# Attention and ternary feed-forward block: q and k projected from two float16 parts, maxima 11 steps ahead of the scores

## What is computed

```python
q, k, v = n @ Wq, n @ Wk, n @ Wv                 # n = layernorm(x), x is (8, 1024, 256)
q, k = rope(q), rope(k)                          # pairs of columns, cos and sin of the position
p = softmax(q @ k.T / sqrt(256))                 # 16 heads, each 1024 x 1024
x = x + layernorm((p @ v) @ Wo)
x = x + layernorm(layernorm(x) @ ternary(W).T * alpha + bias)
```

## Time and profile before

| | before |
|---|---|
| median of 3 runs | 1544.87 us (1544.76 to 1545.48) |
| profiled execution | 1542.89 us, of which the span from first to last instruction is 1540.9 us |
| busy PE / DVE / ACT / POOL | 94% / 88% / 81% / 45% |
| mean granted TensorE clock | 0.979 |

### The profile page before, as it was taken

The page is one execution under the profiler, slowest core; times in us unless marked ns, Lnnn a source line. Parts: engine busy times, 40 slices in busy tenths (PEclk is TensorE's granted clock), DMA queues, the critical chain, the costliest instruction groups (busy, mean ns, idle before and its releaser), DMA issues.

```text
span 1540.9 us, 31812 instructions
## 1 busy us (share of the span) xinstructions
PE 1453.7 (94%) x12182; PEld 481.2 (31%) x12182; DVE 1360.0 (88%) x1565; ACT 1246.7 (81%) x2454; POOL 686.8 (45%) x1115
## 2 busy tenths in 40 slices
PE   6789999999999999999999999999999999999997
PEld 5122322323232332323223232323323232222236
DVE  5788999898989999899998989899998989999924
ACT  2078888888988888888888889888888888989881
POOL 4214074544636355453735446363554535333240
PEclk9589999999999999999999999999999999999999
DMA  3411111312031121312112120301212120220101
GB/s 106 116 26 56 62 28 61 81 46 69 27 101 27 60 57 44 94 33 74 26 61 81 47 69 27 104 24 60 57 46 65 33 78 22 61 50 17 40 16 52
DMA packets 72919, 84.89 MB, mean 55 GB/s; under 512 B 17632, under 2 KB 58464, under 8 KB 71328
## 3 DMA queue, kind: packets, MB, share of 16 engines
q1 hardware_dynamic: 71952, 82.08, 18.8%
q10 hardware_dynamic: 816, 0.79, 0.2%
HBM read 46.66 MB, written 24.64 MB: 46 GB/s over the span
## 4 chain that ended last, share of the span: by engine, by line
PE 46%; DVE 38%; POOL 7%; ACT 4%; issue 3%; DMA 1%; SPq 0%; POOLq 0%; DVEq 0%; ACTq 0%
DVE row_max L1161 31%; PE smax L933 16%; PE pv L955 14%; PE ring L1053 4%; PE ring L1026 4%; ACT probs L835 3%; PE ring L1061 2%; PE ring L1041 2%; PE ring L979 2%; POOL act L423 2%; POOL res L503 2%; DVE sy_bn L1141 1%; PE ring L1003 1%; DVE max_parts L1179 1%; POOL sa_rs L398 1%
## 5 line engine op out<-in xcount | busy, mean ns | idle before, releaser
L1161 DVE TENSOR_REDUCE row_max<-smax 128x1 f32<-128x1024 f32 x1024 | 1206.2, 1215 | 108.5 <-PE smax L933 105.7
L835 ACT ACTIVATE probs<-ring 128x512 f32<-128x512 f32 x2048 | 1104.6, 597 | 167.2 <-PE ring L979 153.3
L933 PE MATMUL smax<-k_rows,q_rows 48*128 48x512 f16 x2048 | 629.4, 389 | 50.3 <-DVE row_max L1161 40.3
L979 PE MATMUL ring<-q_rows,k_rows 50*128 50x512 f16 x2048 | 634.2, 383 | 0.5 <-ACT probs L835 0.2
L955 PE MATMUL pv<-probs,v_cols 128*32 128x256 f32 (+1 forms) x6240 | 603.5, 459 | 4.1 <-ACT heads L889 3.7
L933 PEld LDWEIGHTS smax<-k_rows,q_rows 48*128 48x128 f16 x2048 | 116.7, 94 | 550.7 <-DVE row_max L1161 291.0
L955 PEld LDWEIGHTS pv<-probs,v_cols 128*32 128x32 f32 x6240 | 123.2, 108 | 307.3 <-issue 163.2
L979 PEld LDWEIGHTS ring<-q_rows,k_rows 50*128 50x128 f16 x2048 | 132.2, 93 | 45.1 <-ACT probs L835 39.8
L535 POOL TENSOR_TENSOR attnT<-pairs,inv_rows 128x512 f32<-128x512 f32 x31 | 39.4, 1271 | 235.3 <-DMA inv_rows<-inv_sums_dram 235.3
L514 POOL TENSOR_TENSOR act<-act,bias_sb 128x256 f32<-128x256 f32 x60 | 42.3, 727 | 80.1 <-ACT act L878 80.1
L1026 PE MATMUL ring<-xT,wq_sb 128*128 128x256 f32 x256 | 71.9, 407 | 5.1 <-ACT rot_in L820 5.1
(11 more groups left out here) (155 smaller groups left out, 1099.0 us busy)
## 6 DMA issues: line engine op xcount, KB each, us to landing
q_stage_dram<-q_parts SPq DMA_DIRECT2D x45, 256.0 KB, 2.5
q_rows<-q_stage_dram SPq DMA_DIRECT2D x30, 384.0 KB, 7.8
x_in<-in_L_attn_x SPq DMA_DIRECT2D x8, 1024.0 KB, 6.1
pairs<-heads SPq DMA_DIRECT2D x64, 128.0 KB
inv_rows<-inv_sums_dram SPq DMA_DIRECT2D x32, 256.0 KB
res<-in_L_attn_x SPq DMA_DIRECT2D x16, 512.0 KB, 5.6
out<-res SPq DMA_DIRECT2D x15, 512.0 KB, 3.2
k_rows<-k_stage_dram SPq DMA_DIRECT2D x64, 96.0 KB, 3.3
```

Source lines behind the costliest of these rows:

```text
L835: eng.activation(probs[:, s % PSLOTS, j, :], ring[:, n % RING, :], ACT.Exp, scale=score_unit).then_inc(ring_read, 1)
L933: mm = eng.matmul(smax[:, side, c, :], q_rows[at:to, qc, kv * KVP + jp, qt * P:(qt + 1) * P], k_rows[at:to, kv, c * 512:(c + 1) * 512], st ...
L979: eng.matmul(ring[:, n % RING, :], k_rows[at:to, g, kt * P:(kt + 1) * P], q_rows[at:to, h.qc, g * KVP + j // 2, :], start=True, stop=True)\
L1161: eng.tensor_reduce(row_max[:, g % 2, at:at + 1], smax[:, side, :, :].rearrange("p c n -> p (c n)"), AX.X, ALU.max).then_inc(max_read, 1)
```

## The change

- The x of each batch (scaled by 1024) and the weights of q and k (scaled by 64) are split into two float16 parts (`x_parts`, `wq_parts`, `wk_parts`), on POOL: four `split_x` in steps 1 to 4 of each `qc` 0 half, `split_weights` once. `Q` and `K` are sums of three float16 products (`PRODUCTS`), in jobs of 512 columns: two `Q` jobs, in steps 16 and 30, instead of four in 4 to 7, and one `K` job in step 6 instead of two in 14 and 15.
- q is rotated at step 8 of the half that follows its projection, staged at step 14 and loaded at 16 of that same half.
- `LEAD` is 11, so `TURN` is 6: `MT` stands in steps 6, 14, 22 and 30.
- The cast of `act_parts` goes from DVE to POOL. The first operation of `split_max` becomes a `scalar_tensor_tensor` with a tile of zeros. The moments of x are taken two in a step (0 to 3), those of y all in step 16, and those of the forward result in 27 and 30.

```diff
-LEAD = 12
+LEAD = 11
 TURN = (-LEAD) % KT + 1
...
 PRO = {0: [("XT", 0, 0)], 1: [("XT", 1, 0)], 2: [("XT", 0, 1)], 3: [("XT", 1, 1)],
-       4: [("Q", 0, 0, 0)], 5: [("Q", 0, 0, 1)], 6: [("Q", 0, 1, 0)], 7: [("Q", 0, 1, 1)],
-       14: [("K", 0)], 15: [("K", 1)]}
+       6: [("K",)], 16: [("Q", 0, 0)], 30: [("Q", 0, 1)]}
...
-        4: [("Q", 1, 0, 0)], 5: [("Q", 1, 0, 1)], 6: [("Q", 1, 1, 0)], 7: [("Q", 1, 1, 1)]}
+        16: [("Q", 1, 0)], 30: [("Q", 1, 1)]}
...
-X_MOM_FIRST, X_MOM = (0, 1, 2, 5, 6, 7, 8, 8), (0, 1, 2, 3, 4, 5, 6, 7)
-A_MOM, Y_MOM, F_MOM = (9, 10, 11, 12), (15, 15, 16, 16), (27, 27, 29, 30)
+X_MOM_FIRST, X_MOM = (0, 1, 2, 5, 6, 7, 8, 8), (0, 0, 1, 1, 2, 2, 3, 3)
+A_MOM, Y_MOM, F_MOM = (9, 10, 11, 12), (16, 16, 16, 16), (27, 27, 30, 30)
...
-K_SWAP = 17
+K_SWAP = 18
...
-Q0_STAGE, Q1_STAGE, Q_LOAD = 30, 30, 6
+Q_STAGE, Q_LOAD, Q_LOAD_FIRST = 14, 16, 6
...
+        def split_x(eng, h, n):
...
+            eng.tensor_copy(hi, src).then_inc(x_high, 1)
+            eng.wait_ge(x_high, before + 1)
+            eng.tensor_tensor(lo, src, hi, ALU.subtract).then_inc(x_parted, 1)
...
-        def split_act(eng, nth, dt):
-
+        def split_act(eng, h, nth, dt):
+
+            eng.wait_ge(ring_read, h.done("HT", dt))
+            eng.tensor_copy(act_parts[:, 0, dt, :], actT[:, dt, :]).then_inc(act_part, 1)
...
+                        for k, (xm, wm) in enumerate(PRODUCTS):
+                            for dt in range(DT):
+                                mm = eng.matmul(dst[:, :], wq_parts[:, wm, dt, a[1], :], x_parts[:, xm, dt, at:at + HALF],
+                                                start=(k + dt == 0), stop=(k == len(PRODUCTS) - 1 and dt == DT - 1))
...
-                eng.tensor_scalar(m1, rows, 1.0 / ROW_UNIT, None, ALU.mult).then_inc(max_split, 1)
+                eng.scalar_tensor_tensor(m1, rows, 1.0 / ROW_UNIT, zeros[:, :, :], ALU.mult, ALU.add).then_inc(max_split, 1)
```

More of the change, by code:

```diff
@@ L114 @@
 SPLIT_ALL = sum(SPLIT_OPS)
-def turn_of(row, what):
-    return (("K", "Q0", "Q1") if row <= 1 else ("Q0", "K", "Q1")).index(what)
 def rot_at(row, what):
-    return row * ROT_ALL + sum(6 if w else 3 for w in ((0, 1, 1) if row <= 1 else (1, 0, 1))[:turn_of(row, what)])
+    return row * ROT_ALL + {"K": 0, "Q0": 3, "Q1": 9}[what]
 def split_at(row, what):
-    return row * SPLIT_ALL + 2 * turn_of(row, what)
+    return row * SPLIT_ALL + {"K": 0, "Q0": 2, "Q1": 4}[what]
 JOIN_OPS = 8
@@ L134 @@
 ACT_UNIT = 1024.0
+X_UNIT = 1024.0
+W_UNIT = 64.0
 class Half:
     def __init__(self, b, qc, scores=True, maxima=STEPS, turned=range(1, HKV + 1), pro=None, pro1=None,
-                 epi=None, late=None, base=0, first=0, steps=STEPS, load_x=None, mom=None, flush=True,
+                 epi=None, late=None, rot=None, base=0, first=0, steps=STEPS, load_x=None, mom=None, flush=True,
                  after=()):
@@ L185, in jobs @@
         if self.pro is not None:
-            out += (PRO_FIRST if self.early else PRO).get(s, [])
+            out += (PRO_ALONE if self.alone else PRO_EARLY if self.early else PRO).get(s, [])
         if self.pro1 is not None:
@@ L240, in sandwich_kernel @@
         xT = sb("xT", [P, DT, S], F32)
+        x_parts = sb("x_parts", [P, 2, DT, S], F16)
         rot_in = sb("rot_in", [P, 2, 2, HALF], F32)
@@ L462, in rotate_q @@
             before = rot_at(row, Q_HALF[a])
-            eng.wait_ge(ring_read, h.done("Q", a, 1, 1) if h.scores else h.base)
+            eng.wait_ge(ring_read, h.base)
             at_least(eng, rot_step, before)
@@ L563, in between @@
                     split_k(eng, h.pro, rot_out[:, 0, :])
[L564 to L567, removed]
+                if s in h.x_split:
+                    for n in h.x_split[s]:
+                        split_x(eng, h, n)
+            if h.rot is not None and s == Q_ROT:
+                rotate_q(eng, h, *h.rot)
+                split_q(eng, *h.rot)
+            if h.pro1 is not None and s == 1 - LEAD:
                 rotate_q(eng, h, h.pro1, 1)
                 split_q(eng, h.pro1, 1)
+                split_weights(eng)
             if h.epi is not None:
@@ L636, in swap_k @@
             def swap_k(h):
-                eng.wait_ge(ring_read, h.done("K", 1))
+                eng.wait_ge(ring_read, h.done("K", 1) if h.alone else h.done("K"))
                 for tile in range(4):
@@ L709, in half @@
                         spread_inverses(h, INVERT[s])
[L710 to L716, removed]
+                    if s == Q_LOAD_FIRST and h.very_first:
                         load_q(h.b, 1)
+                    if h.rot is not None and s == Q_STAGE:
+                        stage_q(*h.rot)
+                    if h.rot is not None and s == Q_LOAD:
+                        load_q(*h.rot)
                     if h.turns(s):
@@ L817, in stage_first_q, with move, columns @@
                                   q_parts[:, part, :, 0, :]).then_inc(q_staged[0], 16)
-            def move(dst, src):
-                eng.activation(dst, src, ACT.Copy).then_inc(ring_read, 1)
+            def move(dst, src, unit=1.0):
+                eng.activation(dst, src, ACT.Copy, scale=unit).then_inc(ring_read, 1)
+            def columns(part):
+                return (part[0] * HALF // 2, (part[0] + 1) * HALF // 2) if part else (0, HALF)
             def half(h):
@@ L855, in copy_jobs @@
                             eng.wait_ge(rot_step, rot_at(h.pro - 1, "K") + 2)
[L856 to L857 removed]
+                        at, to = columns(a)
+                        move(rot_in[:, 0, 0, at:to], src[:, 0:to - at], 1.0 / (X_UNIT * W_UNIT))
                     elif kind == "Q":
@@ L1235, in half @@
                         if now := due(s, Y_MOM):
-                            eng.wait_ge(y_added, nth_epi * ST + sum(now))
                             if now[0] == 0:
                                 eng.wait_ge(y_norm, RAISED + nth_epi * (ST + 1))
-                            moments(res, st_y, y_mom, *now)
+                            for t in range(now[0], sum(now)):
+                                eng.wait_ge(y_added, nth_epi * ST + t + 1)
+                                moments(res, st_y, y_mom, t, 1)
                             if h.alone and sum(now) == ST:
```

93 lines of the change are left out of this document (66 added, 27 removed).

## The result

The changed kernel takes **1686.3 us** (median of 4 runs, 1684.5 to 1693.0), 1.092 times the kernel before (95% interval 1.090 to 1.094): 141 us slower, where 54 were forecast. The profiled execution has a span of 1685.1 us against 1540.9.

A forecast was written before the change was run, and what follows sets the result against it. No single engine was taken as the limit: PE bounds steps with a job, DVE those without. Savings of -39 plus stalls of +35, +48 and +10 gave +54 us, thus 1599 us, range 1556 to 1630.

The forecast's parts named there:

- The saving, -39: Whole kernel: moved q and k jobs, DVE's relief and the first batch together save 39 us before any stalls.
- q's return: Steps 16 and 30: the two new Q jobs cost 0.7 us a half together, +9 us over 13 halves.
- DVE's relief: Steps 20 to 23: two casts leave DVE for POOL, saving 0.2 us a half, -3 us.
- The first batch: Half 0: fewer Q and K jobs and one step fewer of maxima ahead of the first score, -4 us.
- The ordinary stall, 0.75: Each group's first score: PE waits 0.75 us because the turn is one step nearer; 47 places outside step 24, +35 us.
- Rival A: First scores: PE is far enough ahead to hide the stalls and step 24's order costs nothing; 1509 us, chance 0.11.
- Step 24, 3.0 a place: Step 24's first score: SP sends the maxima only after step 22's reciprocals; 16 places of 3.0 us, +48 us.
- Rival B: Step 22: DVE's reciprocal is early enough that SP's order there is cheap; 1551 us, chance 0.13.
- The load of x, +10: Step 6 of five halves: x's and the residual's loads stand before the maxima, 2 us each, +10 us.
- Rival C: All the maxima's DMAs queue behind larger ones, making every stall longer; 1632 us, chance 0.14.
- PE thus stands: Each group's first score: PE stands 0.5 to 0.9 us waiting for the maxima, and everything behind it too.
- The operation with two inputs: First operation of split_max: stays at 0.17 us by the row; by the contention rule the total would be 6 us higher.

The follow-up runs named there:

- the kernel with 18 matmuls: The changed kernel plus 18 unread float16 matmuls of 512 columns on PE before the wait for the maxima at step 24 of each half: 1648.3 us.
- the fastest kernel: The changed kernel with the turn at steps 5, 13, 21, 29, x's load at 8, residual's at 7, last pair's reciprocals at 3: 1510.0 us.
- with the maxima first: The changed kernel with one edit: at step 22 SP sends the group's maxima before it waits for the softmax reciprocals: 1599.0 us.
- the kernel with the distance alone: The changed kernel, turn kept at 6, 14, 22, 30, with maxima before reciprocals at step 22, residual at 7, x at 8, last reciprocals at 3: 1552.4 us.

## Why the prediction was right or wrong

The runs form a ladder from the old kernel to the new one, each rung one group of edits (medians):

| rung | us | difference | forecast |
|---|---|---|---|
| before | 1544.9 | | |
| the change with the turn right behind the last maximum (the distance of before), nothing large ahead of the maxima | 1510.0 | -35 | -39 |
| turn a step later against the score | 1552.4 | +42 | +47 |
| x, residual and reciprocals of step 4 in front of the maxima and `WO` | 1599.0 | +47 | +10 |
| reciprocals in front of the maxima at step 22, PE's clock kept | 1648.3 | +49 | +36 |
| the clock | 1686.3 | +38 | none |

(The prediction's 35 and 48 are split here as 63 ordinary stalls of 0.75, and 16 x 2.25 on top of them at step 24.) The rungs add to 141, 87 more than the 54 forecast: +4, -5, +37, +13 and +38. The kernels were measured in different rounds, in which the kernel before had medians of 1542.5 to 1545.0; by the ratios to it in the same round the rungs are -34, +42, +44, +53 and +36, so each is sure to some 4 us. Each price holds in the company of those above it; the kernel with 18 matmuls still has some PE time at half clock in steps 8 and 9.

*The saving, -39: the sum right, its terms less so.* In the fastest kernel (by its trace, whose span is 30.6 us below that of before), over halves 1 to 13, steps 4 to 7 are 33.2 us shorter than before; with the `K` job of step 6 taken off, as the prediction has it, 40.3 - 6.6 = 33.7. Steps 12 to 15 are 8.3 shorter, where the two `K` jobs were given 7.8. Steps 16 to 19 and step 30 are 20.5 longer, 0.79 for each `Q` job, and I had given q's return 9: the cover by the moments of y and of the result, which took that from up to 1.1 a job to 0.35, is there only in part. DVE's relief, 3, was placed in steps 20 to 23, which are 0.3 longer; steps 24 to 29 and 31, for which I had nothing, are 10.0 shorter, so the errors cancel in part, by luck. What shortens those steps no run separates, but for the 2.7 us of DVE's instructions and the 3.4 in steps 26 to 29 that come with eleven steps instead of twelve. The first batch gives 2.6 us ahead of the first score and takes 1.9 back in steps 0 to 3 of half 0, against 4.

*The ordinary stall, 0.75, right.* It was 0.67 to 0.69, and the way to it held: 3.1 us from `MT` to the score. Rival A's premise, that PE would be ahead enough, fell; its number, 1509, is met by the fastest kernel, but by having the turn a step earlier and so no stall.

*Step 24, 3.0 a place, mis-sized.* Step 23 grew by 51.2 us in 13 halves, 3.9 each, beyond even the upper bound of 3.5, which came from the spread's data. SP's order was as the prediction had it, with the issues of the maxima 2.7 us behind `MT`; they landed later than they do alone: the chain has 2.62 us behind the start of SP's second issue (842.45), which I had put at 1.8, and with the maxima first the same DMA took 1.78:

```profile
795.96 1.78 DMA q_rows<-max_rows
```

Rival B fell with it: the reciprocal was not early.

*The load of x, +10, mis-sized.* It measured 47 with the residual and `attnT`. It said that half 8 would lose 0.75 to 3.5 us; that half's step 7 took 5.49 us against 2.21 in the fastest kernel, 2.6 beyond the ordinary stall and inside these bounds, but step 8 behind it took 4.67, partly at the low clock, against 3.13. By the same comparison as above some 21 of the 47 us are the clock's, in step 8, and 27 the stand's, in step 7. And I counted five halves only: half 7, with the residual's load and none of x, has 3.73 in step 7, against 2.36 in the fastest kernel, 0.7 beyond the ordinary stall. With the turn early, the two loads gave back 16.5 us and the reciprocals of step 4, which bring `attnT` and so `WO`, 14.5; I had let that wait hide a stall and given it no price. Rival C had the mechanism, in the wrong place: not all of the maxima, but those of steps 6 and 22, stand behind larger transfers.

*The step that failed is the one that is missing.* "PE thus stands" was priced as time in which PE does nothing, at full clock behind it. Before, PE stood over 2 us four times behind its first instruction, all in the first 110 us; in the changed kernel it did so 28 times, and behind the one read above the clock fell to 0.51 for 7 us. The mean over the run went from 0.979 to 0.935. TensorE: Matmul & The Clock Gate, section Part 1: The HAM clock gate, of the Trainium skill says that a gate lets through a share of the clock's pulses by how busy the array is; the trace agrees, with 0.51 behind such a stand and 1.00 where the gap was filled. The forecast knew of stands of 3 us and didn't ask what the clock does behind them. In its place the runs show 38 us at step 24, which filling the gap takes away, and some 21 at step 8 in the rung of the loads, together about 59 of the 87 us that the forecast fell short. The rest is mostly the longer waits for the maxima's DMAs, 16 at step 8 beyond the 10 forecast and 13 at step 24.

*The operation with two inputs.* I held the row, 0.17 us, against the rule of GPSIMD Engine Reference, section Specifications, of the Trainium skill, that DVE contends with GpSimd also when it reads two SBUF inputs. The trace of the changed kernel sides with the rule:

```profile
736.50 1.28 POOL L463 TENSOR_TENSOR rot_mul<-rot_in,cs_k 128x512 f32<-128x512 f32 x1
...
736.61 1.21 DVE L1241 SCALAR_TENSOR_TENSOR max_parts<-row_max,max_parts 128x16 f16<-128x16 f32 x1
```

The operation of 0.17 us takes 1.21, until POOL's ends (737.82 and 737.78). It began 0.11 us behind POOL's, while that of the earlier trace rows began 0.01 ahead (855.17 against 855.18), so that row did not bear on the question. It cost nothing in sum: the 64 pairs of operations took 14.2 + 15.9 us, against 20.3 + 11.4 before.

## What to carry to other kernels

Where a transfer feeds the engine that bounds a kernel, look at what its queue issues in the few microseconds ahead of it, small waits and large loads alike: here the places of four issues (x, the residual, and the reciprocals of steps 4 and 22) were worth 47 + 49 = 96 us, more than all the arithmetic that the change removed. Price a stall of TensorE twice, as the time it stands and as the slower clock behind it; filling the gap with unread matmuls shows how much of each a kernel pays. And before a lead is shortened, list every wait that it covered, not only the one beside the edit.

## What was not expected of the hardware

- A stand of 3.3 us, in a stream in which PE was 90% busy, was followed by 7.00 us at a granted 0.51. Stalls of 0.7 us (the kernel with the distance alone) left it at 1.00 there, and its mean at 0.979. With 13 matmuls in the gap the clock held in steps 24 and 25 of 7 halves of 16, with 18 in 14.
- The length of the stand alone did not decide. With the maxima first, PE's idle time in step 7 was over 2 us in nine halves, and in all nine steps 8 and 9 had 0.64 to 0.78; of the idle times of 1.09, 1.20, 1.61 and 1.63 us the first and third were followed by 0.78 and 0.64, the others by 1.00. In the changed kernel one of 2.43 (half 14) was followed by 1.00.
- The DMA of the maxima, 2.5 us from issue to score alone, took 3.4 behind the reciprocals' (841.74 to 845.11) and 5.1 behind 1.5 MB of loads.
- A `scalar_tensor_tensor` of 16 columns beside POOL's `tensor_tensor` of 512 took 1.21 us instead of 0.17.
